# The token lists of the routing phase: 96 columns a matmul, products cut by route, remainders on GpSimd

## The reference

```python
def route(x, routing_token, num_tokens, k_eff):
    s = jnp.einsum('bnd,rd->brn', x, routing_token)[:, 0]
    scores = coor_descent(s, k_eff)
    sel_scores, sel_idx = jax.lax.top_k(scores, num_tokens)
...
sq, iq = route(x, rt_q, NQ, min(NQ * FETCH_K, SEQ))
skv, ikv = route(x, rt_kv, NKV, min(NKV * FETCH_K, SEQ))
xq = x[batch_idx, iq]
xkv = x[batch_idx, ikv]
routed_out = heavy_attn(xq, xkv, skv, rms_g, w_q, w_kv, null_kv, w_out)
```

## Time and profile before

| | us |
|---|---|
| median of 3 runs | 4434.96 |
| the three runs | 4431.64, 4434.96, 4438.22 |
| span of the profiled execution, first to last instruction | 4433.8 |
| median less span | 1.2 |
| routing phase, first mask to the last of the lists' operations | 2856.8 to 2917.4 |

### The profile page before, as it was taken

One profiled execution on the slowest core, in us unless ns is written; L12 is line 12 of the kernel. 1 busy time (PEld: TensorE's weight loads), 2 busy tenths in 40 slices (PEclk: granted clock), 3 DMA queues, 4 the chain that ended last, 5 costly groups with the idle time before them and its releaser, 6 DMA issues. The chain is left out here.

```text
span 4433.8 us, 92598 instructions
## 1 busy us (share of the span) xinstructions
PE 4163.1 (94%) x37152; PEld 3493.5 (79%) x37152; DVE 2886.4 (65%) x5096; ACT 1849.9 (42%) x4838; POOL 875.9 (20%) x661
## 2 busy tenths in 40 slices
PE   5788879999999999999999999689999999999999
PEld 5777757888888888788888888577878878788777
DVE  9888867767676677755555666746464564645645
ACT  7444323434344444344444332325354453544534
POOL 0222102222222222212222222210110101101001
PEclk9999879999999999999999999879999999999999
DMA  8688742222222222211211211220220202112010
GB/s 309 165 234 232 211 141 79 92 82 90 82 92 80 91 82 92 65 58 59 68 58 61 65 58 48 90 57 6 51 49 15 53 8 51 37 24 52 12 41 13
DMA packets 341355, 360.63 MB, mean 81 GB/s; under 512 B 23104, under 2 KB 237376, under 8 KB 340928
## 3 DMA queue, kind: packets, MB, share of 16 engines
q1 hardware_dynamic: 262592, 287.52, 21.6%
q0 software_dynamic: 12288, 33.56, 3.6%
q10 hardware_dynamic: 66048, 33.56, 2.8%
HBM read 228.21 MB, written 76.02 MB: 69 GB/s over the span
## 5 line engine op out<-in xcount | busy, mean ns | idle before, releaser
L1683 POOL TENSOR_TENSOR l_prob<-l_prob,l_inv 128x768 f32<-128x768 f32 x256 | 389.6, 1543 | 1691.9 <-DVE l_inv L1640 1691.9
L1234 ACT ACTIVATE l_prob<-l_ps_s,l_neg_max 128x192 f32<-128x192 f32 x1024 | 419.7, 442 | 7.5 <-DVE l_neg_max L1616 7.3
L2294 DVE TENSOR_REDUCE h_neg_max<-h_ps_s 128x1 f32<-128x1024 f32 x256 | 312.9, 1222 | 167.2 <-PE h_ps_s L2080 165.5
L2215 ACT ACTIVATE h_prob<-h_ps_s,h_neg_max 128x1024 f32<-128x1024 f32 x256 | 285.3, 1115 | 279.5 <-DVE h_neg_max L2297 279.5
L1616 DVE TENSOR_REDUCE l_neg_max<-l_ps_s 128x4 f32<-128x768 f32 x256 | 233.2, 952 | 236.9 <-PE l_ps_s L1003 218.0
L2092 PE MATMUL h_ps_t<-ident,h_prob 128*128 128x128 f32 x2048 | 272.7, 276 | 14.6 <-ACT h_prob L2215 14.2
L2092 PEld LDWEIGHTS h_ps_t<-ident,h_prob 128*128 128x128 f32 x2048 | 228.2, 140 | 62.1 <-issue 27.7
L2351 DVE COPY h_probs_t<-h_ps_t 128x512 f32<-128x512 f32 x256 | 176.9, 691 | 124.7 <-PE h_ps_t L2092 123.8
L2104 PEld LDWEIGHTS h_ps_o<-h_probs_t,ahead_then_values 128*64 128x64 f32 x4096 | 220.9, 137 | 43.2 <-issue 37.0
L2104 PE MATMUL h_ps_o<-h_probs_t,ahead_then_values 128*64 128x128 f32 x4096 | 251.8, 276 | 0.0
L1234 ACT ACTIVATION_READ_ACCUMULATOR l_prob<-l_ps_s,l_neg_max 128x1 f32 x1024 | 235.5, 230 | 0.0
(11 more groups left out here) (385 smaller groups left out, 11136.5 us busy)
## 6 DMA issues: line engine op xcount, KB each, us to landing
toep_back<-taps_padded ACTq DMA_DIRECT2D x32, 1024.0 KB, 10.6
x<-xg SPq DMA_DIRECT2D x64, 512.0 KB, 8.7
l_xin<-x SPq DMA_DIRECT2D x128, 256.0 KB, 3.2
l_xres<-x SPq DMA_DIRECT2D x128, 256.0 KB, 3.1
l_val_side<-l_val SPq DMA_DIRECT2D x256, 128.0 KB, 3.1
out_dram<-l_res SPq DMA_DIRECT2D x128, 256.0 KB, 2.0
ahead_then_values<-x SPq DMA_DIRECT2D x126, 256.0 KB, 3.1
xin<-in_L_attn_x_dram SPq DMA_DIRECT2D x32, 768.0 KB, 6.4
```

The costliest lines, as they stand in the source:

```text
L1234: last = nc.scalar.activation(prob[t % 2][:, h, pair, :], ps_s[:, h, pair, BOTH], ACT.Exp, bias=neg_max[:, t % 2, h, pair:pair + 1], accum ...
L1683: nc.gpsimd.tensor_tensor(mine, mine, spread(inv[:, t % 2, h, :], [1, PAIRS], [0, WIN + P]), ALU.mult).then_inc(p_normed, 1)
L2215: nc.scalar.activation(prob[i % 2][:, :].rearrange("p (a k) -> p a k", a=2), ps_s[i % 2][:, :, :], ACT.Exp, bias=neg_max[:, qt % 2, h:h + ...
L2294: nc.vector.tensor_reduce(at, ps_s[i % 2][:, :, :].rearrange("p a k -> p (a k)"), AX_X, ALU.max, negate=True).then_inc(max_step, 1)
```

## The change

Four things are changed, all in `routing_phase` and its helper `heavy_weights`.

- `in_block` becomes the twelfth part of `what`, and each matmul streams 96 = 12 x 8 columns. The eight further columns of the result are not read; the copies still take 88.
- The masks are made route by route (two comparisons of 128x8x128), and so are the products: eleven for the first route ahead of the first row, the eleven for the second route two by two behind the comparisons of rows 0 to 5. TensorE waits for 11 products before rows 0 to 7 and for 22 before rows 8 to 15.
- ScalarE scales the loaded weights in place (three activations) and then rounds them (three more), six where there were three.
- The remainders, now rounded half subtracted from the scaled weight, are made by GpSimd, three a slice, as soon as ScalarE has finished the slice.

```diff
@@ -1711,8 +1711,8 @@
     null_hi = sb("hw_null_hi", [P, HEADS], F32R)
     g_col = sb("hw_g", [P, KC])
     g_q = sb("hw_g_q", [P, KC])
-    loaded, null_in, zeroed, g_q_made, hi_made, lo_made, null_hi_made = (
-        sem(f"hw_{n}") for n in ("loaded", "null_in", "zeroed", "g_q", "hi", "lo", "null_hi"))
+    loaded, null_in, zeroed, g_q_made, scaled, hi_made, lo_made, null_hi_made = (
+        sem(f"hw_{n}") for n in ("loaded", "null_in", "zeroed", "g_q", "scaled", "hi", "lo", "null_hi"))
     LOADS, NULLS = 3, 5
 
     def parts(k):
@@ -1751,8 +1751,12 @@
             act.wait_ge(loaded, 16 * LOADS)
             nc.scalar.activation(g_q[:, :], g_col[:, :], ACT.Identity, scale=DH ** -0.5).then_inc(g_q_made, 1)
             act.wait_ge(g_q_made, 1)
-        for hi, _, raw, scale in parts(k):
-            last = nc.scalar.activation(hi, raw, ACT.Identity, scale=scale[:, k:k + 1])
+        for _, _, raw, scale in parts(k):
+            last = nc.scalar.activation(raw, raw, ACT.Identity, scale=scale[:, k:k + 1])
+        last.then_inc(scaled, 1)
+        act.wait_ge(scaled, k + 1)
+        for hi, _, raw, _ in parts(k):
+            last = nc.scalar.activation(hi, raw, ACT.Identity)
         last.then_inc(hi_made, 1)
 
     def nulls_on_scalar(act):
@@ -1761,14 +1765,13 @@
         nc.scalar.activation(w["null_k"][0:DH, :, 0], raw_null[0:DH, :], ACT.Identity).then_inc(null_hi_made, 1)
         nc.scalar.activation(null_hi[DH:P, :], raw_null[DH:P, :], ACT.Identity).then_inc(null_hi_made, 1)
 
-    def on_vector(v, k):
-        v.wait_ge(hi_made, k + 1)
+    def lo_on_gpsimd(pool, k):
+        pool.wait_ge(hi_made, k + 1)
         for hi, lo, raw, scale in parts(k):
-            last = nc.vector.scalar_tensor_tensor(out=lo, in0=raw, scalar=scale[:, k:k + 1], in1=hi.bitcast(F32),
-                                                  op0=ALU.mult, op1=ALU.subtract)
+            last = nc.gpsimd.tensor_tensor(lo, raw, hi.bitcast(F32), ALU.subtract)
         return last
 
-    return on_sync, on_gpsimd, on_scalar, nulls_on_scalar, on_vector
+    return on_sync, on_gpsimd, on_scalar, nulls_on_scalar, lo_on_gpsimd
 
 
 def routing_phase(nc, tables, keep, lists, weights):
@@ -1787,8 +1790,8 @@
         sb, ps, sem = open_tensors(nc, ctx)
         first_token = sb("r_first_token", [P, BATCH])
         total_no = sb("r_total_no", [P, ROWS, HI])
-        in_block = sb("r_in_block", [P, HI, COLS], BF16)
-        what = sb("r_what", [P, PARTS, HI, COLS], BF16)
+        what = sb("r_what", [P, PARTS + 1, HI, COLS], BF16)
+        in_block = what[:, PARTS, :, :]
         one_hot = [sb(f"r_one_hot{i}", [P, P, NCH], BF16) for i in range(2)]
         steps_wide = sb("r_steps_wide", [P, P, NCH], BF16)
         column_b = sb("r_column_b", [P, COLS], BF16)
@@ -1798,9 +1801,10 @@
 
 
         wide_made = sem("r_wide_made")
-        made, what_made, dve, hot_made, list_made, list_kept = (
-            sem("r_" + n) for n in "made what_made dve hot_made list_made list_kept".split())
+        made, what_made, dve, hot_made, list_made, list_kept, parted = (
+            sem("r_" + n) for n in "made what_made dve hot_made list_made list_kept parted".split())
         steps = keep["steps"]
+        ROUTE_COLS = COLS // ROUTES
         column, block_no, parts = tables["column"], tables["block_no"], tables["parts"]
 
         load_weights, part_nulls, round_weights, round_nulls, part_weights = heavy_weights(nc, ctx, *weights)
@@ -1814,17 +1818,20 @@
             def _(pool):
                 nc.gpsimd.iota(first_token[:, :], pattern=[[SEQ, BATCH]], base=0, channel_multiplier=0,
                                allow_small_or_imprecise_dtypes=True).then_inc(made, 1)
+                for k in range(KC):
+                    part_weights(pool, k).then_inc(parted, 1)
+                pool.wait_ge(parted, KC)
                 part_nulls(pool)
 
             @block.tensor
             def _(pe):
-                pe.wait_ge(what_made, 1)
                 for row in range(ROWS):
+                    pe.wait_ge(what_made, PARTS * (row // BATCH + 1))
                     pe.wait_ge(hot_made, row + 1)
                     if row >= 4:
                         pe.wait_ge(list_kept, row - 3)
                     for t in range(NCH):
-                        last = nc.tensor.matmul(ps_list[row % 4][:, 0:PARTS * HI], one_hot[row % 2][:, :, t],
+                        last = nc.tensor.matmul(ps_list[row % 4][:, 0:(PARTS + 1) * HI], one_hot[row % 2][:, :, t],
                                                 what[:, :, :, row * NCH + t], start=(t == 0), stop=(t == NCH - 1))
                     last.then_inc(list_made, 1)
 
@@ -1851,12 +1858,20 @@
                     ins.then_inc(dve, 1)
                     v.wait_ge(dve, done)
 
-                step(nc.vector.tensor_tensor(in_block[:, :, :], spread(block_no, [0, HI], [1, COLS]),
-                                             spread(steps[:, 0:HI], [1, HI], [0, COLS]), ALU.is_equal))
+                def by_route(a, r):
+                    return a[:, r * ROUTE_COLS:(r + 1) * ROUTE_COLS]
+
+                def part_of(m, r):
+                    cols = slice(r * ROUTE_COLS, (r + 1) * ROUTE_COLS)
+                    nc.vector.tensor_tensor(what[:, m, :, cols], in_block[:, :, cols],
+                                            spread(parts[:, cols, m], [0, HI], [1, ROUTE_COLS]), ALU.mult).then_inc(what_made, 1)
+
+                for r in range(ROUTES):
+                    step(nc.vector.tensor_tensor(in_block[:, :, r * ROUTE_COLS:(r + 1) * ROUTE_COLS],
+                                                 spread(by_route(block_no, r), [0, HI], [1, ROUTE_COLS]),
+                                                 spread(steps[:, 0:HI], [1, HI], [0, ROUTE_COLS]), ALU.is_equal))
                 for m in range(PARTS):
-                    last = nc.vector.tensor_tensor(what[:, m, :, :], in_block[:, :, :],
-                                                   spread(parts[:, :, m], [0, HI], [1, COLS]), ALU.mult)
-                last.then_inc(what_made, 1)
+                    part_of(m, 0)
                 v.wait_ge(wide_made, 2)
 
                 for row in range(ROWS):
@@ -1864,8 +1879,8 @@
                         v.wait_ge(list_made, row - 1)
                     nc.vector.tensor_tensor(one_hot[row % 2][:, :, :], spread(column_b[:, row * NCH:(row + 1) * NCH], [0, P], [1, NCH]),
                                             steps_wide[:, :, :], ALU.is_equal).then_inc(hot_made, 1)
-                    if row >= ROWS - 2 * KC and row % 2 == 0:
-                        step(part_weights(v, (row - ROWS) // 2 + KC))
+                    for m in range(2 * row, min(2 * row + 2, PARTS)):
+                        part_of(m, 1)
                 v.wait_ge(list_kept, ROWS)
                 v.wait_ge(made, 1)
```

## The result

Twenty runs of each kernel: 4440.61 us after against 4433.15 before (medians), a ratio of 1.0019 with a 95% interval from 1.0012 to 1.0025. That is 5 to 11 us slower, by its middle inside the 8.9 us that the forecast counts as no change; 4439.1 us had been forecast.

The account below looks back on a forecast made before the run. The prediction took TensorE as the bound inside the routing phase's 41 us, with one chain through the phase. Its terms, -5.7 + 9.8 + 0 = +4.1 us on 4434.96, gave 4439.1 us, range 4418 to 4446.

Parts of the forecast that it names:

- The sum: Whole kernel: start -5.7, GpSimd and VectorE taking turns +9.8, columns 0, together +4.1 us, giving 4439.1 us.
- The start: Ahead of the first list matmul: half masks +0.2, eleven half products -5.9, so TensorE starts 5.7 us earlier.
- The columns: List matmuls: eight extra columns hidden by the 146 ns weight load, cost 0; the ends are 0 and 3.7 us.
- The upper end: List matmuls: if the weight load does not hide the eight columns, a proportional price of at most 3.7 us.
- The turns of GpSimd and VectorE: Rows 3 to 6: a 1.15 us GpSimd pass ahead of each VectorE pass makes rows late, +9.8 us.
- the rival that put no collision at 4429: Routing phase: GpSimd and VectorE do not collide in bf16, low clock, only the start left; 4429.3 us, chance 0.14.
- ScalarE: Routing phase: six activations a slice at 0.62 us delay the copies of rows 1 to 3; nobody waits.
- the two rivals with the clock: List matmuls: clock rises to 2.4 GHz, 0.08 us each; with collision 4430 (chance 0.13), without 4418.2 (0.09).
- the slower rival: Half products do not halve, 1.14 us each; the start gains nothing, +18 us, 4453; chance 0.09.

Follow-up runs that it names:

- the kernel with both undone: Changed kernel with 88 columns a matmul and the remainders back on VectorE; timed 4430.1 us against 4433.5 before, ratio 0.9984 to 1.0002.
- the version with 88 columns: Changed kernel, each matmul streaming 88 columns again, remainders still on GpSimd; timed 4428.1 us against 4433.5 before, ratio 0.9982 to 1.0000.
- The 64 matmuls with weights side by side: Extra matmuls behind the changed kernel's last row, 96 columns 512 bytes apart, weights adjacent in memory; 0.164 us a matmul.
- the pairs: Extra matmuls behind the changed kernel's last row, 88 columns as pairs of neighbours 512 bytes apart; 0.082 us a matmul.
- the 48-column run: 64 extra matmuls behind the changed kernel's last row, 48 columns 512 bytes apart; 0.094 us a matmul.

## Why the prediction came out, point by point

- **The sum came out by luck: two of its three terms were wrong, and their errors cancelled.** Forecast: -5.7 + 0 + 9.8 = +4.1. Measured in the stretch: +4.4; the three terms one by one, each from a kernel of its own, were -5.7, +3.4 and +6.6 (rounded, +4.3).
- **The start**: -5.7 forecast, 10.51 us after the first mask instead of 16.18 measured, -5.7, alone in the kernel with both undone. Masks 1.26 and half products 0.60 us apart, as worked out.
- **The columns**: taken at 0, "the weight load hides them"; they cost 3.4 us in the kernel before and, where nothing stalls, as much with products by route (54.6 against 51.2). This is the step that failed. The upper end, in proportion to the columns (3.7), was near the truth, and the matmuls stood 0.174 us apart, not 0.160. That 146 + 14 ns gave 0.160 us was accident: the same loads stood 0.094 us apart with 48 columns. The text had named the strided operands, with the Trainium skill's note on lines (SBUF — State Buffer, "Door 1: The DMA port swizzle"), as what would make it 3.7, and had then gone by the load's row and by the pace of 512 columns that lie side by side.
- **The turns of GpSimd and VectorE**: the mechanism was right in bf16 too, and so was the price of a turn (1.15 us forecast, 1.12 to 1.17 measured; comparisons of 2.2 to 2.3 us, half products of 1.78). The size was not: 9.8 forecast, 6.1 us of standing still measured, 6.6 by the difference of the stretches. The forecast let the turns begin as soon as GpSimd had work, and had rows 3 to 6 late by 1.8, 3.25, 3.25 and 1.5 us. The turns began at VectorE's first pause, so row 3 had one turn ahead of it, not two, and was not late at all; rows 4 to 6 were late by 2.6, 2.9 and 1.2, in part because TensorE's longer rows gave VectorE 0.2 us more a row. Had the columns been free, as taken, the pause would have come two rows later and the stalls would have cost 1.4 us, not 9.8. That is the version with 88 columns, -4.3, near the rival that put no collision at 4429: on the forecast's own premise its sum would have had the wrong sign.
- **ScalarE**: its six activations a step delayed its copies and nobody waited, as said. **The clock** stayed at 0.50 (window 2871.90 to 2922.80), so the two rivals with the clock fell. The half products did halve, so the slower rival fell too.
- **The rest of the measured difference.** The timed runs say +5 to +11 us, the stretch +4.4. In the two profiled executions the phase ahead of the first mask was 4.6 us longer and all behind the last matmul 5.0 us shorter; other kernels of the set scatter in the same way. Whether some us outside the stretch belong to the change stays open.

## What to carry to other kernels

Price a matmul's moving operand by the 16 bytes that it opens (here 1.8 to 2.0 ns each) where that is more than its columns cost: where the columns of a matmul lie apart in memory, pack them in pairs in the layout before tuning who makes them. Work handed to GpSimd beside two-input VectorE instructions is free only where VectorE waits anyway: start it behind the stage in which VectorE has no slack, or give VectorE buffers enough not to pause there. Two edits that each look independent can set each other's price through the moment at which an engine first waits, so run each alone and both together.

## What the runs showed of the hardware that I had not expected

- A GpSimd pass that alone takes 1.28 us stood open for 6.96 and 11.91 us beside VectorE instructions that followed each other without a gap, and none of these took longer for it until VectorE's first pause. The Trainium skill (SBUF — State Buffer, "Who interferes with whom") says that whoever issues first holds the shared ports and the other is blocked; that a queue without gaps keeps them from one instruction to the next is what these rows add.
- What a strided column costs doesn't follow the clock. The 64 matmuls with weights side by side ran 0.163 to 0.165 us apart both in the window 2954.2 to 2957 (clock 1.00) and in the one from 2957 to 2964 (0.55), and the pairs 0.08 us apart at 0.50 and at 1.00. So the forecast's two rivals in which the clock doubled TensorE's pace could not have come true with this layout, even with the clock up.
- Two weight loads can overlap: each is 146 ns long in the 48-column run, whose matmuls are 0.094 us apart, one load to each.
